# Two-input forms for three small VectorE instructions, and row transposes first in each attention step on TensorE

## What is computed

```python
x = x + xattn(ctx, ctx, layernorm(x))      # 16 heads of 16, softmax over 64 keys, Wo, bo
x = x + ffn(layernorm(x))                  # sum of two parts:
#   two shared experts (256 -> 512 gelu -> 256), their mean
#   top 2 of 8 routed experts by a gate, weighted by the softmax of the two gate values
```

## Time and profile before

| | |
|---|---|
| median of 3 runs | 382.69 us (381.83 to 383.19) |
| the profiled execution's own time | 382.79 us |
| its span, first to last instruction | 381.1 us |
| mean granted TensorE clock | 0.957 of full |
| TensorE busy | 332.8 us (87% of the span) |
| VectorE busy | 234.7 us (62%) |
| ScalarE busy | 222.6 us (58%) |
| GpSimd busy | 201.2 us (53%) |
| attention stage, to the first shared-expert matmul | to 112.22 us |
| routed experts on TensorE | from 231.96 us |

### The profile page before, as it was taken

The page is one execution under the profiler, slowest core; times in us unless marked ns, Lnnn a source line. Parts: engine busy times, 40 slices in busy tenths (PEclk is TensorE's granted clock), DMA queues, the critical chain, the costliest instruction groups (busy, mean ns, idle before and its releaser), DMA issues. The chain is left out here.

```text
span 381.1 us, 8081 instructions
## 1 busy us (share of the span) xinstructions
PE 332.8 (87%) x2297; PEld 279.3 (73%) x2297; DVE 234.7 (62%) x483; ACT 222.6 (58%) x405; POOL 201.2 (53%) x238
## 2 busy tenths in 40 slices
PE   5979989877678999989799658999999999999970
PEld 4757666645457888969689535898999999999860
DVE  0589999999734429694455232565666666566650
ACT  1265567865749646646456414666667676776650
POOL 4326799999737900387377210335554445445542
PEclk9998999998989999999899957999999999999997
DMA  8960000060006201047552643245544544554332
GB/s 267 399 237 1 3 0 31 28 236 0 3 0 233 101 1 57 27 144 211 160 183 88 207 128 135 33 69 85 82 67 78 83 75 72 85 84 63 53 42 28
DMA packets 23929, 36.92 MB, mean 97 GB/s; under 512 B 4400, under 2 KB 18096, under 8 KB 23504
## 3 DMA queue, kind: packets, MB, share of 16 engines
q1 hardware_dynamic: 16000, 25.06, 20.4%
q0 software_dynamic: 7456, 10.04, 15.4%
q10 hardware_dynamic: 432, 1.31, 1.0%
HBM read 23.21 MB, written 13.19 MB: 96 GB/s over the span
## 5 line engine op out<-in xcount | busy, mean ns | idle before, releaser
L945 POOL DMA_INDIRECT out<-y,xg x39 | 61.0, 1564 | 68.6 <-DVE y L1009 51.6
L691 DVE TENSOR_TENSOR h_lo<-g,h_hi 128x512 fp32r<-128x512 f32 x32 | 24.4, 764 | 51.4 <-PE psS L855 26.2
L1063 PE MATMUL ps<-w_lo,hh_hi 128*128 x156 | 47.1, 302 | 3.5 <-DVE hh_lo L1015 3.5
L996 DVE TENSOR_TENSOR hb<-ps,b1T 128x512 f32<-128x512 f32 x39 | 27.0, 691 | 36.5 <-PE ps L1052 36.0
L855 PE MATMUL psS<-s_lo,h_hi 128*128 128x256 f32 x128 | 37.8, 295 | 9.5 <-DVE h_lo L691 9.5
L1063 PE MATMUL ps<-w_hi,hh_lo 128*128 x156 | 44.0, 282 | 0.0
L1063 PE MATMUL ps<-w_hi,hh_hi 128*128 x156 | 43.6, 280 | 0.0
L487 ACT ACTIVATE g<-psP,sb1T 128x512 f32<-128x512 f32 x32 | 22.0, 687 | 34.6 <-PE psP L841 34.5
L381 POOL TENSOR_TENSOR Pr<-Pr,inv 128x1024 f32<-128x1024 f32 x16 | 30.4, 1902 | 19.1 <-DVE inv L682 19.1
L970 ACT ACTIVATE g<-hb 128x512 f32<-128x512 f32 x39 | 24.7, 632 | 26.9 <-DVE hb L996 26.9
L855 PE MATMUL psS<-s_hi,h_lo 128*128 128x256 f32 x128 | 36.9, 288 | 0.0
(11 more groups left out here) (181 smaller groups left out, 913.1 us busy)
## 6 DMA issues: line engine op xcount, KB each, us to landing
wraw<-in_w SPq DMA_DIRECT2D x16, 512.0 KB, 5.7
xg<-xg_d SPq DMA_DIRECT2D x39, 130.0 KB, 2.4
sraw<-in_sw SPq DMA_DIRECT2D x2, 1024.0 KB, 11.0
out<-xres SPq DMA_DIRECT2D x4, 512.0 KB, 3.5
xres<-in_x SPq DMA_DIRECT2D x3, 512.0 KB, 9.5
xTs<-in_xT SPq DMA_DIRECT2D x3, 512.0 KB, 10.1
xg_d<-filler SPq DMA_DIRECT2D x8, 128.0 KB
b_bc<-in_b SPq DMA_DIRECT2D x1, 1024.0 KB, 6.0
```

The source lines that it names most:

```text
L691: V.tensor_tensor(out=h_lo[:, n % 2], in0=g[:, n % 2], in1=h_hi[:, n % 2].bitcast(F32), op=ALU.subtract).then_inc(hlo_done, 1)
L945: pool.indirect_dma_start(out, bass.IndirectOffsetOnAxis(ap=xg[:, t % NXB, D:D + 1].bitcast(U32), axis=0), y[:, t % NYB], None, compute_op ...
L996: V.tensor_tensor(out=hb[:, n % 2], in0=ps[:, 4 + n % 2].rearrange("p (c n) -> p c n", c=HC), in1=b1T[:, bass.ds(e, 1), :].squeeze(1).unsq ...
L1063: last = nc.tensor.matmul(ps[:, 6 + n % 2, 0:D], a[:, n % 2, c], b[:, bass.ds(e, 1), C * HF + c * D:C * HF + (c + 1) * D].squeeze(1), star ...
```

## The change

Three instructions on VectorE (L523, L654, L655) were `tensor_scalar` with an immediate. They become `tensor_tensor` with a broadcast of a 128x1 tile, `eps` or `minus`, that holds the same number. GpSimd fills the two tiles, and the counts waited for on `masks` rise by two. On TensorE the row transposes of tile s-7 move from behind the output projection to the front of the step, ahead of scores(s+1).

```diff
-        half = sb("half", [P, 1])
+        half, eps, minus = sb("half", [P, 1]), sb("eps", [P, 1]), sb("minus", [P, 1])
...
             pool.memset(half[:], -0.5).then_inc(masks, 1)
-            pool.wait_ge(masks, 4)
+            pool.memset(eps[:], EPS).then_inc(masks, 1)
+            pool.memset(minus[:], -1.0).then_inc(masks, 1)
+            pool.wait_ge(masks, 6)
...
-            pool.wait_ge(masks, 7)
+            pool.wait_ge(masks, 9)
...
-            pool.wait_ge(masks, 8)
+            pool.wait_ge(masks, 10)
...
-            act.wait_ge(masks, 4)
+            act.wait_ge(masks, 6)
...
-            act.wait_ge(masks, 9)
+            act.wait_ge(masks, 11)
...
-                V.tensor_scalar(out=ve1[:, b * TPB:(b + 1) * TPB], in0=mv1[:, b * TPB:(b + 1) * TPB, 1], scalar1=EPS, scalar2=None,
-                                op0=ALU.add).then_inc(ve1_done, 1)
+                V.tensor_tensor(out=ve1[:, b * TPB:(b + 1) * TPB], in0=mv1[:, b * TPB:(b + 1) * TPB, 1], in1=eps[:].to_broadcast([P, TPB]),
+                                op=ALU.add).then_inc(ve1_done, 1)
...
-            dve.wait_ge(masks, 9)
+            dve.wait_ge(masks, 11)
...
-                    V.tensor_scalar(out=ve2[:, t - 1:t + 1], in0=mv2[:, t - 1:t + 1, 1], scalar1=EPS, scalar2=None, op0=ALU.add).then_inc(ve2_done, 1)
-                    V.tensor_scalar(out=nm2[:, t - 1:t + 1], in0=mv2[:, t - 1:t + 1, 0], scalar1=-1.0, scalar2=None, op0=ALU.mult).then_inc(ve2_done, 1)
+                    V.tensor_tensor(out=ve2[:, t - 1:t + 1], in0=mv2[:, t - 1:t + 1, 1], in1=eps[:].to_broadcast([P, 2]), op=ALU.add).then_inc(ve2_done, 1)
+                    V.tensor_tensor(out=nm2[:, t - 1:t + 1], in0=mv2[:, t - 1:t + 1, 0], in1=minus[:].to_broadcast([P, 2]), op=ALU.mult).then_inc(ve2_done, 1)
...
             for s in range(FIRST_CHUNK + CHUNKS + 1):
+                if 7 <= s < NT + 7:
+                    t = s - 7
+                    pe.wait_ge(rows_done, t + 1)
+                    pe.wait_ge(ot_sb, min(s - 3, NT))
+                    for c in range(C):
+                        last = T.transpose(psA[:, c * P:(c + 1) * P], row(t)[:, c * P:(c + 1) * P], ident[:])
+                    last.then_inc(x2t_psum, 1)
                 if s + 1 < NT:
                     scores(s + 1)
                 if 4 <= s < NT + 4:
...
                     last.then_inc(att_psum, 1)
-                if 7 <= s < NT + 7:
-                    t = s - 7
-                    pe.wait_ge(rows_done, t + 1)
-                    pe.wait_ge(ot_sb, min(s - 3, NT))
-                    for c in range(C):
-                        last = T.transpose(psA[:, c * P:(c + 1) * P], row(t)[:, c * P:(c + 1) * P], ident[:])
-                    last.then_inc(x2t_psum, 1)
```

## The result

| | before | after |
|---|---|---|
| median of the runs side by side | 382.31 us (4 runs) | 391.26 us (4 runs, 389.79 to 392.14) |
| the profiled execution | 382.79 us | 391.48 us |
| first shared-expert matmul | 112.22 us | 121.25 us |
| granted TensorE clock, 60 to 100 us | 0.96 | 0.87 |
| VectorE busy, 60 to 100 us | 39.85 us | 28.33 us |

The ratio of after to before is 1.0213, with a 95% interval of 1.0173 to 1.0254. The kernel is slower by 2.1% by this ratio, by 8.95 us between the medians and 8.7 us between the profiled executions; forecast were 4.5. All of it lies ahead of the shared experts: from their first matmul to the end the two profiled executions take 268.88 (before) and 268.55 us (span less start).

The account below looks back on a forecast made before the run. VectorE looked like the attention stage's bound; with the change, a ScalarE and TensorE loop of 6.11 us a step. Eight steps +3.0 and later steps +1.5 gave 382.79+4.5 = 387.3 us, range 384.2 to 391.4.

Parts of the forecast that it names:

- The sign and the mechanism: Attention stage: slower, chance 0.87; transposes wait for rows, closing a loop of ScalarE 2.88, TensorE 3.17, handoff 0.06: 6.11 us.
- TensorE's clock falls in the new gaps: Rival: TensorE idles about 1.8 us before its transposes in steps without queries; one drop costs 1.4 us, 388.7; chance 0.16.
- the many falls: The clock rival's case of a drop in all five gaps, s=8, 10, 12, 13, 14: 394.3 us, outside the range.
- Start of s=7: First row transposes on TensorE: nothing moves up to there, they stay at 48.57 us.
- Eight steps: From s=7 to s=15: eight periods of 6.11 are 48.9 us, against 45.86: +3.0.
- s=15: Step without scores: old length plus what projection adds between transposes and values, 0.40+1.05-0.94 = +0.51 us.
- s=16 and s=18: Later steps, projection now between transposes and values: +0.51 us each.
- s=17: Values there wait for a copy queued behind ScalarE's table load, which hides the added time: 0.
- The forms: VectorE's three small instructions as two-input ones: no gain given, since their wait no longer decides anything in the new order.
- The forms wait as long as today: Rival: VectorE's new forms wait like the old beside GpSimd, at most +2.4 us, 389.7; chance 0.06.
- Faster: GpSimd becomes the bound: Rival: rows always ready, loop open, eight steps shrink to GpSimd's 43.83 busy us: 380.8 us; chance 0.06.
- No change: Rival: new forms wait as the old, VectorE stays the bound, the order costs only what waits hid: 382.8; chance 0.06.

Follow-up runs that it names:

- e3: The changed kernel with twelve identity transposes put before the wait for the rows, in steps following one without queries: 386.86 us, ratio to before 1.0066.
- e1: The kernel before with only the row transposes moved to the front, the old tensor_scalar forms kept: 391.68 us, ratio to before 1.0223.
- e5: The changed kernel with ScalarE making the rows ahead of its PT copy: 380.89 us, ratio to before 0.9966.
- e14: The row transposes first as in the change, but the small forms as one-input reductions; e11's kernel run again: 392.77 us, ratio to before 1.0242.
- e2: The kernel before with only the new two-input forms and memsets, the old order kept: 383.0 us, ratio to before 1.0002.
- e8: The kernel before, old order, with the small forms as reductions that read one input: 379.36 us, ratio to before 0.9920.
- e9: The kernel before with forms as reductions, row transposes between scores and projection, and ScalarE's rows ahead of its PT copy: 378.86 us, ratio to before 0.9896.
- e4: The changed kernel with the row transposes one place later, between scores and projection: 383.14 us, ratio to before 1.0008.
- e11: The row transposes first as in the change, with the small forms as reductions, on a slower chip state: 400.1 us against 384.06 of before, no ratio.

## Why the prediction was right, and where it was short

**The sign and the mechanism** held. The transposes wait for the rows in every step, the wait for x2T ahead of the values is gone from the eight steps, and the period without a clock drop is 6.07 us (6.05 to 6.17 in e3), forecast 6.11. e1 shows that the order alone does it, e3 the period, e5 that ScalarE's four instructions are its other half: with the PT copy out of the circle the period falls to 5.11 and 5.23 in steps without queries.

**The size** was off: +8.95 us between the medians and +8.7 between the profiled executions, forecast +4.5. The step that failed is "TensorE's clock falls in the new gaps", which I kept out of the sum as a rival with a chance of 0.16. It fell in s=7, 9, 11, 13 and 15, five times in one execution. I priced a drop at 1.4 us from probability transposes and scores; it costs 1.6 (7.67 less 6.07), since scores, projection and values all run slow. By e3 it is 6.2 us in the eight steps and by the medians 4.4 of the whole (391.26 less 386.86), since in e3 the clock fell later on instead. What misled me is one stretch of the earlier trace rows, from 98 to 100 us, where TensorE did little (0.44 of 2 us) and the clock stood at 1.00: I let it weigh as much as the fall to 0.50 at 86 us. The gaps I forecast at 1.8 us (1.92 to 2.03 measured) were longer than that of 1.16 which had been followed by a fall, and there were five new ones. That should have made some falls the main case.

**That the time lies within the range** is luck. The range ended at 391.4; the median is 391.26 and the profiled execution 391.48. Its upper end stood for long pitches and two falls of the clock, and it left the many falls out, for which I had 394.3. The pitches were those of the sum and the falls were five, four of them in the eight steps (6.2 us) and one in s=15. What kept the time below 392 has nothing to do with my reasons: the first transposes came 0.88 us early, and s=17 took 1.26 us less.

**The rest of the sum**, term by term. Start of s=7: 0 forecast, -0.88 measured. It does not go with the order: with the new one s=7 starts at 47.69 (after), 48.04 (e3) and 48.42 (e14), with the old one at 48.57 (before), 47.99 (e2) and 48.24 (e8). What moves it is open. Eight steps: +3.0, and e3 measures +3.06. (The 45.86 us of before hold one fall of the clock, that of the earlier trace rows; the forecast took them as they were, and so does the +3.06.) s=15: +0.51, measured 4.90 less 4.58 = +0.32 in e3, +1.49 after, with a fall of the clock (0.50 from 104 to 106 us). s=16 and s=18: +0.51 each, measured +0.23 each: I added 0.40+1.05-0.94, and in s=16 it is 0.28+0.96-1.00. Without scores between them the transposes-to-projection pitch is 0.28 us (108.84 to 109.12) and the projection-to-values pitch 0.96, and before the step from transposes to values was 1.00 there. s=17: 0 forecast, -1.26 measured. The time before held a low clock there (0.55 from 106 to 108 us), which the execution of after did not. The order does not decide that: in e3, with the new one, the same step took 7.40 us, in e14 6.09.

**The forms.** The forecast gave them nothing in the new order: right (e14). My reason was wrong in one part. I took from the L691 row that a two-input form waits "for one GpSimd instruction and not for two"; e2 shows 2.84 us through parts of two, 2.88 before. By my value the form of 0.15 us could not have lasted more than about 2.1. In the old order the waits did cost something, 2.8 us of the eight steps by e8. For the kind of form the runs decide. With two inputs in e2, L656 took 2.84 and 3.50 us, waits that went on through the next GpSimd instructions; as a reduction in e8 it took 0.13 us beside L337, and no instance there is slow (0.13 to 0.16 us).

**The rivals.** "The forms wait as long as today" was right about the forms in the old order and wrong about the time: in the new order the eight of L656 took 5.7 us over 20 to 130 us against 10.6 in e2, with GpSimd busy less of the time beside them (44.35 of 55.08 us, before 43.83 of 45.86), and they lie in time that VectorE spends waiting anyway. "Faster: GpSimd becomes the bound" did not come with this change; e9 came near it, at 378.9, once the loop was shorter. "No change" is what e2 and e4 measured, each half of the change put where it does no harm.

## What to carry to other kernels

When an instruction moves to the front of an engine's step (here scores, projection and values stood up to 2.03 us behind the wait of the transposes), ask which engine makes its input and what that engine must do first; if part of that is work of the same step, the two no longer overlap, and the sum around the circle is the new period. Then look at the gaps that the new wait leaves on TensorE: here gaps of 1.9 to 2.0 us cost another 1.6 us each in most cases (four of the five in the eight steps of after), twice as much in the eight steps as the wait itself (6.2 against 3.1), and twelve idle transposes took that back for as long as they were put in. And where a small VectorE instruction is sometimes 20 times as long as at its shortest (3.53 against 0.17 for L654), look for GpSimd work beside it; here a reduction in its place never waited. Expect gain only where VectorE's end is waited for: 2.8 us of 9.0 here.

## What the runs showed of the hardware that was not expected

- A two-column VectorE `tensor_tensor` beside GpSimd took 2.84 us in e2 where its shortest took 0.16, through the rest of one GpSimd instruction and the whole of the next, and another 3.50 us, through the rest of one and two whole ones. The old `tensor_scalar` did the same in before (2.88 and 3.53). A large two-input one waited 1.11 us, inside one pair. Reductions over the same numbers took 0.13 to 0.16 in e8.
- TensorE's clock after a gap. The gap of 2.02 or 2.03 us in front of s=9 was followed by a granted clock of 0.50 for 2 to 3 us in all four of these executions (after 62.55 to 65.55, e1 61.27 to 63.27, e11 61.81 to 64.81, e14 61.69 to 64.69). That of 1.92 in front of s=7 was followed by it in the one of after (0.50 from 49.69 to 51.69, step 7.67 us) and not in e14, e1 and e11 (1.00, step 6.08). Gaps of 1.15 and 1.16 in s=13 of e2 and before were followed by a fall (0.58 from 84 to 86 us, 0.50 from 86 to 88), and one of 1.81 in e4, in front of s=13's row transposes, was not (the clock stayed at 1.00 from 80 to 86 us). So the length of the gap alone does not decide it; what else does is left open, no run was made on it.
- In after the fall is as regular as a rhythm: 7.67 and 6.07 us in turn over four pairs. The step with the low clock has queries behind it, its next gap is only 0.20 us, and by then the granted clock is back at 1.00 (66.55 to 67.55 us in s=9); the step after it has no queries, and the long gap comes again. (s=13 and s=14 have no queries, and s=14 has the gap without the fall.)
- Twelve transposes of 128x128 in 1.47 us, ahead of a gap of 0.60, kept the clock at 1.00 over 50 us; two steps behind the last of them it fell.
